# Router sets moved between power steps, two transfers for the second half's first rows, and two tiles at a time in the last stage

## The reference, cut to what matters

```python
# block 1, per batch b
xB = einsum('bsd,de->sbe', x, Bm);  h = scan(h @ A + xB)       # linear recurrence over 256 tokens
importance = softmax(einsum('bsd,bd->bs', x, h_final @ W_imp.T), axis=-1)
token_pref = softmax(einsum('bsd,nd->bsn', x, W_router), axis=-1)          # "router", 64 neurons
neuron_w   = normalised einsum('bs,bsn->bn', importance, token_pref)
shared_compress = einsum('bn,ndr->bdr', neuron_w, compress)                # [16, 256, 128]
scores = (x @ shared_compress) @ K.T / sqrt(128)                           # 8192 keys
out = sum over top 8 of softmax(top8 scores) * V[top8 index]
# block 2: cross attention, 16 heads of 64, mask, clip to [-5, 5]
# block 3: experts: one-hot dispatch (perm), relu(d @ f1 + bias) @ f2, and back through perm
```

## Time and profile before

| | |
|---|---|
| runs | 1381.36, 1380.46, 1378.34 us; median 1380.46 us |
| profiled execution | 1377.7 us |
| its span, first to last instruction | 1375.8 us |
| PE busy in the span | 1321.6 us (96%) |
| DVE, ACT, POOL busy | 1125.4, 718.8, 728.9 us |

### The profile page before, as it was taken

The page is one execution under the profiler, slowest core; times in us unless marked ns, Lnnn a source line. Parts: engine busy times, 40 slices in busy tenths (PEclk is TensorE's granted clock), DMA queues, the critical chain, the costliest instruction groups (busy, mean ns, idle before and its releaser), DMA issues.

```text
span 1375.8 us, 25304 instructions
## 1 busy us (share of the span) xinstructions
PE 1321.6 (96%) x9877; PEld 993.5 (72%) x9877; DVE 1125.4 (82%) x1628; ACT 718.8 (52%) x1377; POOL 728.9 (53%) x1009
## 2 busy tenths in 40 slices
PE   9877999999999999999999999999999999999898
PEld 5455778786878787878787868787878676767775
DVE  2479889898989898989898988898989986546567
ACT  1353655555555555555555555555555544336554
POOL 0554465555565656565655565656565647341434
PEclk9997999999999999999999999999999999999999
DMA  9562121212121212121212121212121216002412
GB/s 368 182 197 65 46 74 54 74 55 74 54 74 55 74 54 74 55 74 54 74 54 74 54 74 54 74 55 74 54 74 44 74 42 182 1 26 84 156 43 83
DMA packets 57557, 110.38 MB, mean 80 GB/s; under 512 B 9446, under 2 KB 38110, under 8 KB 56286
## 3 DMA queue, kind: packets, MB, share of 16 engines
q1 hardware_dynamic: 40350, 62.17, 15.0%
q0 software_dynamic: 14848, 41.96, 10.6%
q10 hardware_dynamic: 2240, 4.63, 0.9%
HBM read 98.50 MB, written 10.22 MB: 79 GB/s over the span
## 4 chain that ended last, share of the span: by engine, by line
PE 88%; DVE 5%; issue 2%; another core or an unknown queue 2%; ACT 2%; DMA 0%; SPq 0%; POOL 0%; POOLq 0%; ACTq 0%; DVEq 0%
PE side_bank L387 51%; PE score_bank L387 33%; PE score_bank L766 2%; DVE cand_idx L1177 1%; DVE cand_val L1174 1%; PE side_bank L766 1%; DVE dispatchedT L1335 1%; PE side_bank L548 1%; ACT exp L922 0%; PE score_bank L606 0%; ACT score_row L910 0%; SPq L318 0%; DVE x_sum L1200 0%; POOL exp L1425 0%
## 5 line engine op out<-in xcount | busy, mean ns | idle before, releaser
L910 ACT COPY score_row<-score_bank 128x512 f32<-128x512 f32 x512 | 298.9, 591 | 112.2 <-PE score_bank L387 56.7
L1397 POOL DMA_INDIRECT v_rows<-in_V,top_idx x256 | 249.0, 973 | 130.8 <-issue 74.5
L1174 DVE MAX8 cand_val<-score_row 128x8 f32<-128x2048 f32 x128 | 291.7, 2279 | 28.6 <-ACT score_row L910 26.3
L1177 DVE FIND_INDEX8 cand_idx<-cand_val,score_row 128x8 uint32<-128x2048 f32 x128 | 292.5, 2285 | 0.0
L1425 POOL TENSOR_SCALAR exp<-exp,exp_bound 128x256 f32<-128x256 f32 x512 | 248.9, 502 | 79.8 <-ACT exp L922 78.1
L387 PE MATMUL score_bank<-keysT_hi,qT_hi 128*128 128x512 f32 x512 | 216.9, 424 | 21.0 <-ACT score_row L910 19.9
L387 PE MATMUL score_bank<-keysT_hi,qT_lo 128*128 128x512 f32 x512 | 204.9, 400 | 0.0
L387 PE MATMUL score_bank<-keysT_lo,qT_hi 128*128 128x512 f32 x512 | 204.7, 400 | 0.0
L922 ACT ACTIVATE exp<-side_bank 128x512 f32<-128x512 f32 x256 | 139.1, 595 | 91.3 <-PE side_bank L387 84.3
L387 PE MATMUL side_bank<-qT_heads,kT 64*128 64x256 f32 x1024 | 145.2, 402 | 2.6 <-ACT exp L922 2.6
L387 PEld LDWEIGHTS score_bank<-keysT_hi,qT_hi 128*128 128x128 f32 x512 | 97.9, 191 | 62.1 <-ACT score_row L910 25.3
(11 more groups left out here) (200 smaller groups left out, 2284.0 us busy)
## 6 DMA issues: line engine op xcount, KB each, us to landing
kT<-den_scratch SPq DMA_DIRECT2D x62, 256.0 KB
f_quads<-in_f POOLq DMA_DIRECT2D x32, 256.0 KB, 3.4
comp_then_wqkv_raw<-in_comp SPq DMA_DIRECT2D x6, 1024.0 KB, 19.0
xT_by_step<-in_xTs SPq DMA_DIRECT2D x4, 1024.0 KB, 9.1
xT_in<-in_xT SPq DMA_DIRECT2D x16, 256.0 KB
keysT_raw<-in_KmT ACTq DMA_DIRECT2D x8, 512.0 KB, 20.2
x_sum<-in_x SPq DMA_DIRECT2D x32, 128.0 KB, 2.0
ctxT_in<-in_ctxT SPq DMA_DIRECT2D x16, 256.0 KB
```

Of the source, the lines that this page charges most:

```text
L910: nc.scalar.copy(srow[n // PER % 2][:, i * CB:(i + 1) * CB], scb[n % 3]).then_inc(sem("score_evac"), 1)
L1174: own(nc.vector.max(cv[:, tile, cs], srow[g % 2][:, :]))
L1177: nc.vector.max_index(ci[:, tile, cs], cv[:, tile, cs], srow[g % 2][:, :]).then_inc(sem("cand_done"), 1)
L1397: pool.indirect_dma_start(out=vg[:, k, :], out_offset=None, in_=V_rows, in_offset=bass.IndirectOffsetOnAxis(ap=i8[:, tile, k:k + 1], axis=0))\
```

## The change

1. **Router sets 0 and 1** stand between the power steps on PE: set 0 ahead of step 2 (in place of a filler, behind waits for `small_in` and `xs_in0`), set 1 behind step 3 (behind a wait for `xs_in1`). `bm_powers(1)` comes ahead of `bm_powers(0)`, which writes a bank of router set 1 and waits for its copy. Step 5 now follows step 4 directly. ACT's and DVE's lists follow.
2. **Ahead of the importance**: all four router transposes stand ahead of the second half of the importance products. DVE finishes router sets 0 to 3 but for one sum ahead of the importance's maximum or directly behind it, so both `token_weights` stand next to each other.
3. **Stores**: the first half's 32 rows go in four transfers (they were eight), and the second half's rows 0 and 1 in two, one for each row, with four source partitions each (they were four, one for each column quarter).
4. **Fillers**: `warm(3)` ahead of the importance's transposes is `warm(5)`, `warm(16)` is `warm(22)`.
5. **Last stage**: PE makes the transposes of two tiles, then the collects of two.

```diff
+        scd_b0 = scd.rearrange("q (o g c w) -> o q c g w", o=2, g=4, c=4)[1]
...
-            for half in range(2):
-                sp.wait_ge(sem("sc_act"), 2 * half + 2)
-                sp.wait_ge(sem("sc_dve"), 2 * half + 2)
-                store_rows(half, 0, KT, "sc0_stored")
-                if half == 0:
-                    store_rows(0, KT, B * KT, "sc_stored")
-            sp.wait_ge(sem("sc0_stored"), 16 * 8)
+            sp.wait_ge(sem("sc_act"), 2)
+            sp.wait_ge(sem("sc_dve"), 2)
+            store_rows(0, 0, "sc0_stored")
+            sp.wait_ge(sem("sc_act"), 4)
+            sp.wait_ge(sem("sc_dve"), 4)
+            for k in range(KT):
+                sp.dma_start(scd_b0[k], scs[k:P:32, CH:2 * CH]).then_inc(sem("sc0_stored"), 16)
+            sp.wait_ge(sem("sc0_stored"), 16 * 6)
             sp.dma_start(sct[:, :, :], scd_v[0]).then_inc(sem("sct_in"), 16)
-            store_rows(1, KT, B * KT, "sc_stored")
+            store_rows(1, KT, "sc_stored")
...
-            for r in range(4):
-                power(r)
-                if r < 3:
-                    warm(1, pp[0])
+            power(0)
+            warm(1, pp[0])
+            power(1)
+            pe.wait_ge(sem("small_in"), 16 * 5)
+            pe.wait_ge(sem("xs_in0"), 16)
+            router(0)
+            power(2)
+            warm(1, pp[0])
+            power(3)
+            pe.wait_ge(sem("xs_in1"), 16)
+            router(1)
...
             pe.wait_ge(sem("pow_evac"), 4)
+            bm_powers(1)
+            pe.wait_ge(sem("router_evac"), 2)
             bm_powers(0)
-            bm_powers(1)
             power(4)
-            pe.wait_ge(sem("ba_evac"), 2)
-            pe.wait_ge(sem("xs_in0"), 16)
-            router(0)
             power(5)
...
             power(7)
-            router(1)
             router_transpose(0)
+            router(2)
+            router_transpose(1)
...
-            warm(16, pp[1])
+            warm(22, pp[1])
...
-            for n in range(-2, NT):
-                if n + 2 < NT:
-                    inter_transpose(n + 2)
-                if n >= 0:
-                    collect(n)
+            for n in range(-2, NT, 2):
+                for i in range(2):
+                    if n + 2 < NT:
+                        inter_transpose(n + 2 + i)
+                for i in range(2):
+                    if n >= 0:
+                        collect(n + i)
... (vector)
+            router_sum(0)
+            router_sum(1)
+            router_recip(0)
             router(2)
-            router_sum(0)
+            router(3)
+            router_sum(2)
             dve.wait_ge(sem("pre_pe"), PRE_PE["imp_pe"])
...
-            router_sum(1)
+            router_sum(3)
...
-            router_recip(0)
+            router_recip(1)
             token_weights(0)
-            router(3)
-            router_sum(2)
-            router_sum(3)
-            router_recip(1)
             token_weights(1)
```

More of the change, by code:

```diff
@@ L449, in _ @@
             pe.wait_ge(sem("bmt_in"), 16)
-            pe.wait_ge(sem("small_in"), 16 * 5)
             pe.wait_ge(sem("pow_evac"), 4)
+            bm_powers(1)
+            pe.wait_ge(sem("router_evac"), 2)
             bm_powers(0)
-            bm_powers(1)
             power(4)
-            pe.wait_ge(sem("ba_evac"), 2)
-            pe.wait_ge(sem("xs_in0"), 16)
-            router(0)
             power(5)
             pe.wait_ge(sem("ba_evac"), 4)
-            for q in range(1, 4):
+            for q in range(2, 4):
                 pe.wait_ge(sem(f"xs_in{q}"), 16)
@@ L472, in _ @@
             last.then_inc(sem("pre_pe"), 1)
-            router(2)
             pe.wait_ge(sem("pre_dve"), PRE_DVE["scan2_evac"])
@@ L859, in router_out @@
                 nc.scalar.copy(rtT[:, n, :], rt_bank[n]).then_inc(sem("router_evac"), 1)
-            for hf in range(2):
-                act.wait_ge(sem("ba_pe"), hf + 1)
+            router_out(0)
+            router_out(1)
+            for n, hf in enumerate((1, 0)):
+                act.wait_ge(sem("ba_pe"), n + 1)
                 for k in range(KT):
@@ L875, in _ @@
             router_exp(0)
+            router_exp(1)
             router_out(3)
             key_hi(1)
-            router_exp(1)
             router_exp(2)
+            router_exp(3)
             act.wait_ge(sem("pre_dve"), PRE_DVE["imp_max"])
@@ L940, in _ @@
                 if c == -1:
[L941 removed]
+                    act.wait_ge(sem("sc_stored"), 16 * 4)
                 for j in range(4):
```

18 lines of the change are left out of this document (6 added, 12 removed).

## The result

The changed kernel took 1371.87 us (median of 4 runs, 1370.52 to 1372.10), the kernel before, on the same chip, 1379.4 (4 runs, 1377.77 to 1381.36). The ratio is 0.9949, interval 0.9934 to 0.9965: 7.5 us faster by the medians (7.0 by the ratio), where 8.9 were forecast.

The account below looks back on a forecast made before the run. PE was taken as 88% of the chain, with time changing only in the first 130 us and last 62; -0.6 - 2.1 - 2.2 - 4.0 = -8.9 off 1380.46 gave 1371.6 us, range 1369 to 1374 (1367.5 to 1376.9 with the cold opening).

Parts of the forecast that it names:

- Last stage, forecast -4.0: Last stage: 15 pairs of joins save 0.32 each, -4.8; one more tile of DVE at the end costs +0.8.
- neither rival on this stage: Last stage: joins save nothing, stage +0.8 (chance 0.04); or ACT's copies gate the pairs, stage +7.4 (chance 0.02).
- Opening, forecast -0.6: Power steps up to the scan: with router sets 0 and 1 among them, the scan starts at 20.6 to 21.9, before 21.8.
- before, it rose only some 3 us into the first long run: Opening: PE's clock before rose only in `bm_powers`, from 15.27, not among power steps and fillers.
- clock stays down: Opening: set 0 takes 3.7 at half clock, power steps stay sparse; opening +3.3, total 1375.5; chance 0.22.
- Together -2.1: Scan to neuron weights: importance maximum 0.8 earlier, joined token weights another -1.3; bounds -1.0 to -2.5.
- Stores and clock, forecast -2.2 for the second row: Stores to second row of scores: read back 2.0 earlier, second row 2.0 to 2.3 earlier, filler and clock included.
- SP free earlier: Stores: four small issues go away, SP is free 1.4 earlier and waits for DVE's copy: -1.0.
- Two issues and not four: Stores: the second transfer begins 0.4 to 0.5 behind the first, where the fourth began 1.2 behind: -0.7.
- stores do not land earlier: Stores: transfers take a microsecond more, or weights are bandwidth-bound; stretch -0.6, total 1373.2; chance 0.10.
- The clock term: Before the first scores: 22 fillers keep PE busy to 66.3; if the clock stays up, first row -2.9 more.
- This does not pass on: First to second row: the clock's -2.9 stops there, as ACT's casts wait for weight pieces that shift by 2.0 only.

Follow-up runs that it names:

- the filled wait: Changed kernel with three fillers more between power step 1 and router set 0, in the wait for x (also "x filled"); 0.9952 of the kernel before.
- the sets in one run: Changed kernel with set 3 split, 30 fillers, two weight pieces first, and router sets 0 and 1 together between power steps 1 and 2; 0.9921, 1360.0 us.
- the split: Changed kernel with half of router set 3 ahead of the wait for DVE's copy of the scan result, half behind the projection; 0.9946, 1370.9 us.
- the repeat: The changed kernel once more, unchanged, on the third chip; 0.9954 of the kernel before, 1364.5 us.
- last stage alone: Kernel before with only the last stage changed, two tiles at a time; 0.9968, 1373.1 us.
- sets alone: Kernel before with only the new order of the router sets, from power steps to neuron weights; 0.9996, 1377.2 us.
- two queues: Changed kernel with router set 3 split and one of the second half's two first-row stores issued by ACT, not SP; 0.9953, 1365.6 us.
- stores alone: Kernel before with only the new stores of the second half's first rows and 22 fillers for 16; 0.9987, 1376.2 us.
- fillers alone: Changed kernel with 30 fillers for 22 between the scores of compression and the read back; 0.9959, 1365.8 us.
- weights first: Changed kernel with set 3 split and two weight pieces loaded ahead of the second half's remaining rows: 0.9927, 1362.1 us; with 30 fillers too: 0.9912, 1358.6 us.

## Why the prediction was right, point by point

**The total** was right, in direction and within its range, with a forecast 1.4 us too large against the medians. That 1371.87 lies so near to 1371.6 is luck in part: the forecast was taken off 1380.46, which is 1.1 above the median with the fourth run in it, and three of its four terms promised too much. By rows, the opening gave +0.4 for -0.6 (medians of all kernels), scan to neuron weights -0.5 for -2.1, the stores -1.0 for -2.2; only the last stage gave what was forecast, and it is over half of the whole.

**Last stage, forecast -4.0: right.** -4.10 in the profile, -4.4 measured alone. Pairs take 3.12, as worked out. PE is busy 40.00 of 40 us and waits for no copy of ACT, so neither rival on this stage holds. The pair of tiles saves 0.34 for the 0.32 of the sum. By the sentence of the Trainium skill ("TensorE: Matmul & The Clock Gate", Part 3, The mechanism) as the rival took it, joined transposes, which share their row groups, would save nothing; the trace disagrees, and its 4.1 us decide.

**Opening, forecast -0.6: right in the pair of profiles (-0.94), wrong as a rule.** I took one execution's clock for the kernel's. Up to the scan all kernels but two (the filled wait, the sets in one run) have one of two instruction lists:

| first product of the scan, us | executions | median |
|---|---|---|
| sets as before | 21.05, 21.17, 21.24, 21.74 | 21.2 |
| sets in the power steps | 20.80, 21.21, 21.23, 21.59, 21.70, 22.44, 24.25, 24.80 | 21.65 |

Here lies a step that failed: "before, it rose only some 3 us into the first long run". In three of the four executions of the old order power step 0 (4.84 us) already had products at full clock (0.43 us for the small one, not 0.68), and the profile of before happened to be the fourth, the slowest. In those three the clock fell again at 8.4 to 8.9 us (`bm_powers` took 3.78 us), so the early rise gained only 0.5 to 0.7 at the scan. So there was less to win than that profile shows. In the new one the rival "clock stays down" came true in two of eight, at +2.5 and +3.1 against the start before, 21.74; it had been given 0.22, and +3.1 to +3.5.

**Scan to neuron weights, forecast -2.1, measured -0.5: the step that failed.** It was "Together -2.1", -0.8 and -1.3. The second half held: from the importance maximum to DVE's last copy it takes 15.17 or 15.18 us in all executions of the joined order, for 16.58 before, -1.4. The first half came out +0.92 (23.73 for 22.81), because PE's list was added up at full clock. The list itself was near right: with the clock held and the wait covered by the split it takes 21.81, -1.00 against before, where the terms without the wait give -1.27 and DVE's lateness +0.2. But with set 1 gone set 2 had moved ahead of scan 2, and nothing dense was left between scan 2 and the projection; the clock falls there, for most of set 3 and the first importance products: 1.92 in five of five, 0.26 of it the wait. No rival of mine had a fall behind the scan; all looked for the clock where it was low already.

**Stores and clock, forecast -2.2 for the second row: measured -1.04** (80.04 - 59.71 = 20.33 for 82.50 - 61.13 = 21.37), -1.2 in the repeat. The read back itself: forecast -2.0, measured -1.15 (-1.14 to -1.18 in every kernel in which SP issues both transfers). SP free earlier: -0.98, as forecast -1.0. Two issues and not four: -0.41 for -0.7, since the first of the two takes 0.72 us, where the old ones took 0.27 to 0.51. The landing, counted from the start of the last issue: +0.23 (3.37 for 3.14) for -0.3; of it that issue itself is 1.59, for 0.70. The last two are the mis-sized terms; the bound (-1.0) just held them. So nearly all of the gain is SP's earlier freedom, and whether the second half's four transfers would have done as well was not run. The rival "stores do not land earlier" priced the stretch at -0.6: the truth was nearer to it than to the forecast.

The clock term was right in its mechanism and did not show in the changed kernel. With 22 fillers the clock held, or it fell ahead of the score products, by execution:

| fillers | first row behind DVE's last copy, us | second row behind it, us |
|---|---|---|
| 16, clock fell (before, last stage alone, sets alone) | 16.8, 17.4, 16.5 | 21.4, 22.0, 21.1 |
| 22, clock fell (changed, its repeat, two queues, x filled) | 15.7, 15.6, 15.8, 15.7 | 20.3, 20.2, 20.4, 20.3 |
| 22, clock held for the product with the rows read back only (stores alone) | 14.5 | 19.6 |
| 22, clock held (split) | 13.0 | 19.8 |
| 30, clock held (fillers alone) | 13.0 | 21.7 |
| weights first, clock held (22; 30 in three) | 12.9; 12.9, 13.1, 13.0 | 17.5; 17.5, 17.7, 17.6 |

Read the two columns side by side: an early first row does not bring an early second one until the weights come first. So the forecast's "This does not pass on" was shown, by the split kernel's idle 2.15 us; that ACT would wait in the changed kernel itself was wrong.

**What stays open:** how the 7.5 us are spread to the last microsecond. The three parts alone add up to -0.6 - 1.8 - 4.4 = -6.8 by the ratios, each with 1.2 to 1.5 of doubt; the whole gives -7.0 and -6.3 by the same measure, so they make it up. The mean parts by rows, +0.4 (opening, by the medians), +0.92, -1.40, -1.1 and -4.1, are -5.3 together, and where the other 1 to 2 us lie isn't known. In the pair of profiles 0.76 is lost between the second row and the last stage. There the profile before is the odd one: 1231.8 us, for 1232.2 to 1232.8 in the changed kernel and the four kernels of the first chip.

## What to carry to other kernels

A sum of PE's list holds only at the clock that the list keeps: before dense products are moved away from a wait, look at what remains around it, since one microsecond of them between two thin steps was worth 1.9 here. An edit that wins on the first item of a queue is worth what the second item can follow; find out what that waits for (here weights queued behind less urgent stores, 2.2 us) and move it in the same change. In a stretch whose clock hangs on how an execution falls, one profile is one draw: compare distances between two events on several kernels before a difference is put down to an edit.

## What the runs showed of the hardware

- With one and the same instruction list the first rise of TensorE's clock came at different times: the small product of power step 0 took 0.43 us at full clock or 0.68 at half, and set 0, from 8.2 to 9.7 us on, took 3.1 to 3.7 us for 1.9 in each execution in which it stood alone. What set 0 ran at, set 1 need not: it took 1.94, or 3.6 and 3.7 where the scan was late.
- Two stretches of the preamble (scan to importance maximum, and from there to DVE's last copy) repeat to 0.01 us between executions and chips (23.73, 21.81, 15.17). The stretch from the second row of scores to the last stage, whose instructions no edit touches, does not: 1232.2 to 1232.8 us on the first chip, 1224.8 to 1225.7 on the second, 1222.8 to 1225.1 on the third. There lie the 7 us between the chips.
- Issuing a store from four partitions, 32 apart, took SP 0.72 us and a second one right behind it 1.59, ACT 1.11; a store of two neighbouring ones took SP 0.23 to 0.70. Two weight pieces of one queue landed 1.3 us apart in one kernel and 3.2 in another.
